# A graph transformer layer with a sparse expert step on one core: gap work, scatter-adds by halves, and a first expert product in three passes

## The chip, the cores and the metric

The kernel runs on one core of a Trainium2 chip. The metric is device time in microseconds. Engines are named as in the profile: PE (TensorE), PEld (its weight load), DVE (VectorE), ACT (ScalarE), POOL (GpSimd), SP (SyncE).

## The reference

1250 nodes of 768 features, 21,250 edges (self loops included). x is normalized (xn); to x are added a graph network and an attention by positive features, both of xn; then a layer of 8 experts, each token through its best two.

```python
# graph network, of xn
x_norm = layer_norm(x, norm_g, norm_b)
out1 = gat_conv(x_norm, src, dst, W1, a_src1, a_dst1, b1, 4, 192, n)   # 4 heads
out2 = gat_conv(out1, src, dst, W2, a_src2, a_dst2, b2, 2, 96, n)      # 2 heads
gnn = concat([x, out2]) @ Wu + bu
# gat_conv
h = (x @ W).reshape(n, H, C)
e = leaky_relu((h * a_src).sum(-1)[src] + (h * a_dst).sum(-1)[dst], 0.2)
ee = exp(e - segment_max(e, dst)[dst])
out = segment_sum(ee / segment_sum(ee, dst)[dst] * h[src], dst)
# experts, y = layernorm(x)
p = softmax(y @ router_w.T);  top 2, divided by a balance, normalized
out = sum over the two experts of gate * silu(y @ w1[e].T) @ w2[e].T
x = x + out
```

## The kernel before, in words

Nodes are kept as NT = 10 tiles of 128. The graph's edges become a dense table of counts, `cnt[st]` (source tile x 1280 targets, uint16), built by indirect scatter-adds on POOL. A product in fp32r takes three passes, `mm3`: hi x hi, hi x lo, lo x hi, where `hi` is the fp32r copy of an operand (ACT) and `lo` what is left (DVE, a subtract); a plain `mm` is in fp32. Eight PSUM banks go round in the order of `reserve` (line 302); `take`, `finished` and `evacuated` are the waits on them.

Ahead of the first attention PE computes h1 in 2 x 10 tiles (line 1855 on), half by half, with W1 folded and scaled by the gain. The second half's weights (`A0 + 1`) are split by `split_gain_hi` (ACT) and `split_gain_lo` (DVE, after the bias product `wb`). Between the h1 tiles PE turns the count table into mask tiles (`mask_tile`, at `PEN_AT`), which ACT makes into `pen[dt]`. For each head h and target tile dt, DVE takes the largest score over the sources, `masked_max`, with two inputs from SBUF: the row of scores `a_row[h]` and `pen[dt]`. Tiles 0 to 3 are taken for all four heads at once, tiles 4 to 9 head by head. `leaky_max` makes of them two columns per target; PE turns these (`max_rows`), DVE copies the result (`mrow`), POOL writes it to `m_d` and reads it back spread over all partitions (`u1_row`, `u2_row`). The rows of head 0 stand where `a_row[1]` and `a_row[2]` were, so they can be loaded only after the maxima of these heads. ACT takes an offset off the ten `cnt` tiles after the last h1 tile.

An attention (DVE's `attention`, line 1353) goes over heads and source tiles: ACT makes `vbuf`, DVE `pbuf` (line 1373), ACT the exponential, DVE times the counts (line 1399), PE ten products for `aggregate` (line 1890). `pbuf` has three buffers. `bank_out` divides a finished head.

Between the attentions PE spreads the new score rows (`aR`), turns Wu's lower part (`wuT`), multiplies it by the router (`wuR`), sums the router (`rsum`), and then takes x1 tile by tile through the router, with `spread_shifts` for the two heads of the second attention; meanwhile DVE does its 20 maxima.

The expert stage has NP_ = 27 tiles of up to 128 rows, each of one expert, `owner[a]`. A tile a: POOL fetches its rows of y from DRAM (`ygot`, line 718), PE turns them (`turn_rows`), ACT copies them (`ygT`), PE multiplies them by the owner's W1 out of `f1_all` (group `F`, 256 columns, fp32), ACT does silu, PE turns the hidden rows (`hT`), DVE copies them (`hgT`), PE multiplies by W2 (group `S`, two halves of 384), DVE scales by the gate into `orow`, and POOL adds these rows to `out` by an indirect DMA (line 728). An addition waits until the one before has landed, since two tiles can hold the same row of `out`. Ahead of it stands a routing part on DVE that makes the lists `fetch`, `send`, `owner` and the gates.

## Time and profile before

| | us |
|---|---|
| median of 3 runs (lowest, highest) | 1066.67 (1063.98, 1069.22) |
| profiled execution, its own time | 1061.51 |
| its span | 1059.8 |
| PE busy | 925.7 (87%) |
| DVE busy | 627.1 (59%) |
| POOL busy | 389.6 (37%) |
| ACT busy | 386.2 (36%) |

The profile is of one execution; the 1.7 us beside the span lie around it. In the chain that ended last PE has 53%, DVE 20%, DMA 16%, waiting for nothing that shows 6%. The mean granted clock of PE is 0.935 of full speed. In the rows below, times are from the span's start; "[x <-E name Ln]" is idle time of the engine ahead of the row and who ended it.

### The profile page before, as it was taken

Reading aid. Unit: us, or ns where it says so; the run is one execution under the profiler, and the core shown is the slowest. Engines: PE = TensorE matmul, PEld = TensorE weight load, DVE = VectorE, ACT = ScalarE, POOL = GpSimd, SP = SyncE. Lnnn points to the kernel's source line nnn. Section 1 sums busy time; section 2 is a strip of 40 time slices with the busy share of each in tenths; the row PEclk is TensorE's granted clock in tenths of the full one; section 3 lists DMA queues with packets and bytes.
Section 4 is the critical chain, followed back from the end, with each engine's and each line's share of the span. In section 5 each row is a group of like instructions: output and inputs, shape, how many; then the busy total and the mean of one; then the engine's idle time right before and its main releaser. Section 6 shows DMA issues by size and latency. Waiting matters only on the chain.

```text
span 1059.8 us, 13855 instructions
## 1 busy us (share of the span) xinstructions
PE 925.7 (87%) x5064; PEld 785.8 (74%) x5064; DVE 627.1 (59%) x1222; ACT 386.2 (36%) x575; POOL 389.6 (37%) x302
## 2 busy tenths in 40 slices
PE   3899899999999999999189999897888469999993
PEld 3798785786678899999088988886877457666672
DVE  7676995602078132386989999695996763222221
ACT  2543330223344000244576766346863401121120
POOL 3058888888888874000110000000000313434441
PEclk9999999969999999999589999989988759999997
DMA  9994579333226449600140000216005924666664
GB/s 315 232 161 83 96 203 263 51 45 45 1 1 145 63 92 287 200 2 1 51 149 23 1 1 1 88 63 208 2 1 199 363 60 91 119 120 119 120 120 60
DMA packets 78417, 112.43 MB, mean 106 GB/s; under 512 B 34994, under 2 KB 53933, under 8 KB 78351
## 3 DMA queue, kind: packets, MB, share of 16 engines
q0 software_dynamic: 35264, 39.86, 22.9%
q1 hardware_dynamic: 40781, 65.39, 19.2%
q10 hardware_dynamic: 2306, 6.29, 1.5%
q8 instruction: 42, 0.69, 0.3%
q14 instruction: 24, 0.20, 0.1%
HBM read 80.02 MB, written 31.49 MB: 105 GB/s over the span
## 4 chain that ended last, share of the span: by engine, by line
PE 53%; DVE 20%; DMA 16%; issue 6%; ACT 2%; SPq 1%; POOL 0%; POOLq 0%; DVEq 0%; ACTq 0%
PE bank L1621 41%; DMA out<-orow,send 14%; PE bank L1890 9%; DVE pbuf L1399 4%; DVE pbuf L1373 3%; DVE sb_before L1318 3%; DVE junk_k L1194 2%; PE bank L1632 2%; DVE h L1382 2%; DMA keyrow<-key_d 2%; SPq L552 1%; DVE o L1382 1%; PE bank L1826 0%; DVE sb_stats L1142 0%; DVE xnT_lo L1118 0%
## 5 line engine op out<-in xcount | busy, mean ns | idle before, releaser
L661 POOL DMA_INDIRECT table<-match_n,slot_ix x168 | 276.2, 1644 | 90.2 <-issue 48.9
L1890 PE MATMUL bank<-h,pbuf 128*128 128x197 f32 (+1 forms) x1200 | 194.5, 324 | 29.6 <-DVE pbuf L1399 28.6
L1890 PEld LDWEIGHTS bank<-h,pbuf 128*128 128x128 f32 x1200 | 186.7, 199 | 37.4 <-DVE pbuf L1399 34.2
L1194 DVE SCALAR_TENSOR_TENSOR junk_k<-keyrow,key,sb_before 128x384 uint8<-128x384 f32 x168 | 92.7, 614 | 21.8 <-DMA keyrow<-key_d 11.5
L1318 DVE CUSTOM_DVE_ANT_0 sb_before<-a_row,pen 128x1280 bf16<-128x1280 f32 x60 | 89.4, 1491 | 27.3 <-ACT pen L958 11.2
L1606 DVE TENSOR_SCALAR orow<-bank,gates 128x384 f32<-128x384 f32 x54 | 33.4, 618 | 115.8 <-PE bank L1621 115.8
L692 POOL IOTA cst_i<- 128x128 int32 x1 | 0.2, 229 | 271.8 <-DVE o L1382 271.8
L1016 ACT ACTIVATE pbuf<-pbuf 128x1280 f32<-128x1280 f32 x60 | 76.1, 1269 | 64.4 <-DVE pbuf L1373 64.4
L1399 DVE SCALAR_TENSOR_TENSOR pbuf<-pbuf,cnt 128x1280 f32<-128x1280 f32 x60 | 88.7, 1485 | 0.0
L1621 PE MATMUL bank<-xnT_hi,w_hi 128*128 128x512 f32 (+1 forms) x216 | 85.1, 394 | 3.7 <-DVE xnT_lo L1118 2.8
L728 POOL DMA_INDIRECT out<-orow,send x27 | 42.9, 1587 | 111.5 <-DMA out<-orow,send 92.5
L1621 PE MATMUL bank<-w_hi,xnT_hi 128*128 128x384 f32 x240 | 82.3, 343 | 0.0
L1621 PE MATMUL bank<-w_hi,xnT_lo 128*128 128x384 f32 x240 | 80.7, 336 | 0.0
L1621 PE MATMUL bank<-w_lo,xnT_hi 128*128 128x384 f32 x240 | 80.5, 336 | 0.0
L1621 PE MATMUL bank<-xnT_lo,w_hi 128*128 128x512 f32 (+1 forms) x216 | 78.3, 363 | 0.0
L1621 PE MATMUL bank<-xnT_hi,w_lo 128*128 128x512 f32 (+1 forms) x216 | 78.2, 362 | 0.0
L1621 PE MATMUL bank<-f_all,ygT 128*128 x324 | 77.0, 389 | 1.2 <-issue 0.7
L1621 PE MATMUL bank<-f_all,hgT 128*128 x216 | 74.3, 487 | 1.3 <-DVE hgT L1587 1.3
L1373 DVE SCALAR_TENSOR_TENSOR pbuf<-u_row,sb_scol,vbuf 128x1280 f32<-128x1280 f32 x40 | 61.7, 1550 | 12.7 <-PE bank L1890 12.3
L1621 PEld LDWEIGHTS bank<-f_all,ygT 128*128 128x128 f32 x324 | 61.1, 195 | 9.5 <-issue 1.9
L815 ACT ACTIVATE kq<-bank,sb_kqb_c 128x512 f32<-128x512 f32 (+1 forms) x36 | 22.2, 617 | 112.0 <-PE bank L1621 104.6
L1098 ACT ACTIVATE hrow<-bank 128x256 f32<-128x256 f32 x27 | 10.4, 384 | 131.2 <-PE bank L1621 131.2
(346 smaller groups left out, 1668.4 us busy)
## 6 DMA issues: line engine op xcount, KB each, us to landing
...
```

What stands on the lines that cost most here:

```text
L661: pool.indirect_dma_start(table[i], bass.IndirectOffsetOnAxis(ap=slot_ix[:, g:g + 1], axis=0), match_n[:, g:g + 1], None, compute_op=ALU.a ...
L728: pool.indirect_dma_start(out, bass.IndirectOffsetOnAxis(ap=send[:, a:a + 1], axis=0), orow[a % 3][:, :], None, compute_op=ALU.add, bounds ...
L815: step(nc.scalar.activation(kq[j % 2][0][:, 0:w], b[:, 0:w], ACT.Identity, bias=kqb_c[:, col:col + 1]))
L1016: nc.scalar.activation(pbuf[i % 3][:, :], pbuf[i % 3][:, :], ACT.Exp).then_inc(e_done, 1)
L1194: nc.vector.scalar_tensor_tensor(out=junk_k[g % 2][:, :], in0=keyrow[c % KR][:, w:w + KW * P], scalar=key[:, g:g + 1], in1=before[:, first ...
L1318: ins = nc.vector.tensor_tensor_reduce(out=junk_m[:, :], in0=rows_a[h][:, :], in1=pen_t[:, :], scale=1.0, scalar=-3e38, op0=ALU.subtract, ...
L1373: nc.vector.scalar_tensor_tensor(out=pbuf[i % 3][:, :], in0=u1_r[h][:, :], scalar=scol[:, h, st:st + 1], in1=vbuf[i % 2][:, :], op0=ALU.ad ...
L1382: ins = nc.vector.scalar_tensor_tensor(out=out_rows(h, per * i + d), in0=pv[:, d, 0:chans], scalar=rec[:, d:d + 1], in1=added(h, per * i + ...
L1399: nc.vector.scalar_tensor_tensor(out=pbuf[i % 3][:, :], in0=pbuf[i % 3][:, :], scalar=2.0, in1=cnt[st][:, :], op0=ALU.min, op1=ALU.mult).t ...
L1606: ins = nc.vector.tensor_scalar(orow[a % 3][:, hf * HALF:(hf + 1) * HALF], b[:, 0:HALF], gates[:, a:a + 1], None, ALU.mult)
L1621: return nc.tensor.matmul(o, l, r, start=first, stop=last)
L1890: ins = nc.tensor.matmul(b[:, d * stride:d * stride + v.shape[-1]], score[:, dt * P:(dt + 1) * P], v, start=st == 0 and d == 0, stop=st == ...
```

## The change

Ahead of the first attention: mask tiles are made at other h1 tiles, two at a time from the second half on; DVE takes tiles 4 to 9 for heads 0 and 1 together, then for head 2, and head 3's six maxima go into the first attention (`between_first`), as do the sums for the layer's bias. Head 3's shift columns go to `m_d` by a DMA of SP straight from `ucol`. The low part of W1's second half is made by POOL in two passes, and so is the low part of Wu. ACT's work on `cnt` is spread over the second half of h1. Between the attentions: `wuT` and `rsum` come ahead of the `aR` spreads, and ACT takes the second head's shift rows after the attention's third and fourth tiles. In the expert stage: ACT and DVE split the owner's W1 (`own_hi`, `own_lo`) and the turned rows (`ygT_hi`, `ygT_lo`) for every tile, the first product goes through `mm3`, and each tile's rows are added in two indirect DMAs of 384 columns, each waiting for the same half of the tile before.

```diff
+        ygT_hi = [at(f"ygT_hi{i}", (181664, 105472)[i], [P, KD, P], F32R) for i in range(2)]
+        ygT_lo = [at(f"ygT_lo{i}", 61440 + 3072 * i, [P, KD, P], F32R) for i in range(2)]
...
+        own_hi = [at(f"own_hi{i}", (108544, 76800)[i], [P, KD, FI], F32R) for i in range(2)]
+        own_lo = [at(f"own_lo{i}", (114688, 82944)[i], [P, KD, FI], F32R) for i in range(2)]
...
-        PEN_AT = [(0, 2), (0, 4), (0, 7), (0, 8), (1, 0), (1, 1), (1, 2), (1, 3), (1, 4), (1, 5)]
-        ROWS_AT = {(1, 6): 0, (1, 9): 1}
+        PEN_AT = {(0, 2): [0], (0, 3): [1], (0, 4): [2], (0, 6): [3], (1, 0): [4, 5], (1, 1): [6, 7], (1, 2): [8, 9]}
+        ROWS_AT = {(1, 5): 0, (1, 6): 1, (1, 8): 2}
+        LESS_AT = {(1, 3): [0], (1, 4): [1, 2], (1, 5): [3], (1, 6): [4, 5], (1, 7): [6], (1, 8): [7, 8], (1, 9): [9]}
...
+            sp.wait_ge(m_done, H1)
+            sp.dma_start(m_d[2 * (H1 - 1) * NT:2 * H1 * NT, :].rearrange("(k t) p -> p k t", k=2), ucol[:, H1 - 1, :, :],
+                         allow_slow_non_contiguous=True).then_inc(m_out[H1 - 1], 16)
...
+            pool.wait_ge(w_hi_done, SPLITS.index(A0 + 1) + 1)
+            finished(pool, "wb", 1)
+            i, gain = SLOT[A0 + 1], gb_c[:, 0, :].unsqueeze(2).broadcast_to([P, KD, HALF])
+            nc.gpsimd.tensor_tensor(w_raw[i][:, :, :], w_raw[i][:, :, :], gain, ALU.mult).then_inc(gain_done, 1)
+            pool.wait_ge(gain_done, 1)
+            ins = nc.gpsimd.tensor_tensor(w_lo[i][:, :, :], w_raw[i][:, :, :], w_hi[i][:, :, :].bitcast(F32), ALU.subtract)
+            ins.then_inc(w_split, 1)
             for h in range(H1):
-                evacuated(pool, "mT", h)
-                pool.dma_start(m_d[2 * h * NT:2 * (h + 1) * NT, :], mrow[h % 2][:, :]).then_inc(m_out[h], 16)
                 if h == 2:
+                    pool.wait_ge(max_done, NT + NT - 4)
                     pool.dma_start(u1_row[0][:, :], row_of(m_d, 0)).then_inc(u_row_in[0], 16)
                     pool.dma_start(u2_row[0][:, :], row_of(m_d, 1)).then_inc(u_row_in[0], 16)
-                pool.wait_ge(m_out[h], 16)
+                if h < H1 - 1:
+                    evacuated(pool, "mT", h)
+                    pool.dma_start(m_d[2 * h * NT:2 * (h + 1) * NT, :], mrow[h % 2][:, :]).then_inc(m_out[h], 16)
+                if h < H1 - 1:
+                    pool.wait_ge(m_out[h], 16)
             finished(pool, "h1", 1, NT - 1)
...
+                if h == H1 - 1:
+                    pool.wait_ge(m_out[h], 16)
                 pool.dma_start(u1_row[h][:, :], row_of(m_d, 2 * h)).then_inc(u_row_in[h], 16)
                 pool.dma_start(u2_row[h][:, :], row_of(m_d, 2 * h + 1)).then_inc(u_row_in[h], 16)
 
+            pool.wait_ge(g_hi_done, 1)
+            nc.gpsimd.tensor_tensor(wuo_lo[:, :, :], wuo_raw[:, :, :], wuo_hi[:, :, :].bitcast(F32), ALU.subtract).then_inc(g_split, 1)
...
+            def send_rows(a, hf):
                 if a == 0:
                     pool.wait_ge(send_done, 1)
                     pool.wait_ge(out_sent, 16 * NT)
                 else:
-                    pool.wait_ge(added_out, 16 * a)
-                pool.wait_ge(orow_done, 2 * (a + 1))
-                pool.indirect_dma_start(out, bass.IndirectOffsetOnAxis(ap=send[:, a:a + 1], axis=0), orow[a % 3][:, :], None,
-                                        compute_op=ALU.add, bounds_check=N - 1).then_inc(added_out, 16)
+                    pool.wait_ge(added_out[hf], 16 * a)
+                pool.wait_ge(orow_done, 2 * a + hf + 1)
+                pool.indirect_dma_start(half_rows, bass.IndirectOffsetOnAxis(ap=send[:, hf, a:a + 1], axis=0),
+                                        orow[a % 3][:, hf * HALF:(hf + 1) * HALF], None,
+                                        compute_op=ALU.add, bounds_check=2 * N - 1).then_inc(added_out[hf], 16)
...
+                    if (hf, t) == (0, 4):
+                        split_gain_hi(act, A0 + 1)
                     if (hf, t) == (0, 5):
-                        split_gain_hi(act, A0 + 1)
-                    if (hf, t) == (0, 6):
                         weight_rows(1)
-            for i in range(NT):
-                nc.scalar.activation(cnt[i][:, :], cnt[i][:, :], ACT.Identity, bias=less_c[:, 0:1]).then_inc(cnt_done, 1)
+                    for i in LESS_AT.get((hf, t), ()):
+                        nc.scalar.activation(cnt[i][:, :], cnt[i][:, :], ACT.Identity, bias=less_c[:, 0:1]).then_inc(cnt_done, 1)
...
-            rows_out("uR2", (0,), 1, u1_row_b[1])
-            rows_out("uR2", (1,), 1, u2_row_b[1])
-            act.wait_ge(max_done, MAX1 + 2 * NT)
-            attention(H1, H2, u2_row_b, row_ready_2)
+            act.wait_ge(max_done, MAX1 + NT)
+
+            def rows_between(i):
+                if i in (2, 3):
+                    rows_out("uR2", (i - 2,), 1, (u1_row_b, u2_row_b)[i - 2][1])
+
+            attention(H1, H2, u2_row_b, row_ready_2, rows_between)
...
+            def own_weights(a):
+                if a >= 2:
+                    finished(act, "F", a - 2)
+                e = act.value_load(owner[0:1, a:a + 1], min_val=0, max_val=E - 1)
+                nc.scalar.activation(own_hi[a % 2][:, :, :].rearrange("p k n -> p (k n)"),
+                                     f1_all[:, bass.DynSlice(e, 1), :, :].rearrange("p o k n -> p (o k n)"), ACT.Copy).then_inc(own_hi_done, 1)
...
+            own_weights(0)
             turned_rows(0)
+            act.wait_ge(out_sent, 16 * NT)
+            own_weights(1)
...
+                if a + 2 < NP_:
+                    own_weights(a + 2)
...
-                if dt == 0:
-                    for h in range(H1):
-                        dve.wait_ge(a_in[h], 16)
                 masked_max(pen[dt], a_row, range(H1), dt)
-                if dt == 1:
-                    split_gain_lo(dve, A0 + 1)
-            for h in range(H1):
-                for dt in range(4, NT):
-                    if h == 0:
-                        evacuated(dve, "pen", dt, 0), evacuated(dve, "pen", dt, 1)
-                    masked_max(pen[dt], a_row, (h,), dt)
-                dve.wait_ge(max_done, 4 + (h + 1) * (NT - 4))
-                leaky_max(H1, h, 1)
+            def max_row_out(h):
                 b = finished(dve, "mT", h)
                 if h >= 2:
                     dve.wait_ge(m_out[h - 2], 16)
                 nc.vector.tensor_copy(mrow[h % 2][:, :], b[0:2 * NT, 0:P]).then_inc(free("mT", h), 1)
...
+            for dt in range(4, NT):
+                evacuated(dve, "pen", dt, 0), evacuated(dve, "pen", dt, 1)
+                masked_max(pen[dt], a_row, (0, 1), dt)
+            dve.wait_ge(max_done, NT)
+            leaky_max(H1, 0, 1), leaky_max(H1, 1, 1)
+            for dt in range(4, NT):
+                if dt == 7:
+                    max_row_out(0), max_row_out(1)
+                masked_max(pen[dt], a_row, (2,), dt)
+            dve.wait_ge(max_done, NT + NT - 4)
+            leaky_max(H1, 2, 1)
+
+            def between_first(i):
+                if i == 0:
+                    max_row_out(2)
+                if i == 1:
+                    bias_of_layer()
+                if i % 3 == 2 and i < 18:
+                    masked_max(pen[4 + i // 3], a_row, (3,), 4 + i // 3)
+                if i == 18:
+                    dve.wait_ge(max_done, MAX1)
+                    leaky_max(H1, 3, 1)
+
...
-            dve.wait_ge(g_hi_done, 1)
-            nc.vector.tensor_tensor(wuo_lo[:, :, :], wuo_raw[:, :, :], wuo_hi[:, :, :].bitcast(F32), ALU.subtract).then_inc(g_split, 1)
...
+            def low_rows(a):
+                if a >= 2:
+                    finished(dve, "F", a - 2)
+                for h in range(2):
+                    b = finished(dve, "yT", a, h)
+                    dve.wait_ge(y_hi_done, 2 * a + h + 1)
+                    s = slice(3 * h, 3 * h + 3)
+                    nc.vector.tensor_tensor(ygT_lo[a % 2][:, s, :], transposed(b, h), ygT_hi[a % 2][:, s, :].bitcast(F32),
+                                            ALU.subtract).then_inc(free("yT", a, h), 1)
+
+            def own_low(a):
+                e = dve.value_load(owner[0:1, a:a + 1], min_val=0, max_val=E - 1)
+                dve.wait_ge(own_hi_done, a + 1)
+                nc.vector.tensor_tensor(own_lo[a % 2][:, :, :].rearrange("p k n -> p (k n)"),
+                                        f1_all[:, bass.DynSlice(e, 1), :, :].rearrange("p o k n -> p (o k n)"),
+                                        own_hi[a % 2][:, :, :].rearrange("p k n -> p (k n)").bitcast(F32), ALU.subtract).then_inc(own_done, 1)
...
+            dve.wait_ge(owner_done, 1)
+            own_low(0)
...
+            low_rows(0)
...
+            own_low(1)
...
             for a in range(NP_ + 1):
+                if a + 1 < NP_:
+                    low_rows(a + 1)
                 if a:
                     expert_rows(a - 1)
                 if a < NP_:
                     turned_hidden(a)
+                if a + 2 < NP_:
+                    own_low(a + 2)
...
-                    if (hf, t) in PEN_AT:
-                        mask_tile(PEN_AT.index((hf, t)))
-                    if (hf, t) == (0, 6):
+                    for dt in PEN_AT.get((hf, t), ()):
+                        mask_tile(dt)
+                    if (hf, t) == (0, 5):
                         bias_rows(1)
                     if (hf, t) in ROWS_AT:
                         max_rows(ROWS_AT[hf, t])
-            max_rows(2), max_rows(3)
...
-            pe.wait_ge(dots_done, 2)
-            for h in range(H2):
-                spread_row("aR", (), h, scol[:, h, :])
-
...
+            pe.wait_ge(mean_done, 2)
+            b = take(pe, "rsum")
+            for m in range(KD):
+                ins = mm(b[:, 0:EM], ones[:, :], rw_raw[:, m, :], m == 0, m == KD - 1)
+            ins.then_inc(full("rsum"), 1)
+            pe.wait_ge(dots_done, 2)
+            for h in range(H2):
+                spread_row("aR", (), h, scol[:, h, :])
             evacuated_all(pe, "wuT")
-            pe.wait_ge(mean_done, 2)
...
-            b = take(pe, "rsum")
-            for m in range(KD):
-                ins = mm(b[:, 0:EM], ones[:, :], rw_raw[:, m, :], m == 0, m == KD - 1)
-            ins.then_inc(full("rsum"), 1)
...
+                    pe.wait_ge(own_done, a + 1)
                     b = take(pe, "F", a)
                     for k in range(KD):
-                        ins = mm(b[:, 0:FI], ygT[a % 2][:, k, :], f1_all[:, bass.DynSlice(e_of[a], 1), k, :], k == 0, k == KD - 1)
+                        ins = mm3(b[:, 0:FI], [z[a % 2][:, k, :] for z in (ygT_hi, ygT_lo)],
+                                  [z[a % 2][:, k, :] for z in (own_hi, own_lo)], k == 0, k == KD - 1)
                     ins.then_inc(full("F", a), 1)
```

POOL ahead of the first attention, before: the four writes of the shift columns and the loads of the rows.
```order
L681 DMA m_d<-sb_mrow 20x128 [waits bank_free5]
L681 DMA m_d<-sb_srow 20x128 [waits bank_free1,m_out0]
L681 DMA m_d<-sb_mrow 20x128 [waits bank_free2,m_out1]
L683 DMA u_row_137<-m_d 128x1280
L684 DMA u_row_141<-m_d 128x1280
L681 DMA m_d<-sb_srow 20x128 [waits bank_free3,m_out2]
L688 DMA u_row_138<-m_d 128x1280 [waits bank_full0,m_out3]
L689 DMA u_row_142<-m_d 128x1280
```
And now (`w_raw_84` and `w_lo_81` are the second half of W1, one place in memory):
```order
L690 TENSOR_TENSOR w_raw_84<-w_raw_84,sb_gb_c 128x2304 [waits bank_full3,w_hi_done]
L692 TENSOR_TENSOR w_lo_81<-w_raw_84,w_hi_78 128x2304 [waits gain_done]
L701 DMA m_d<-sb_mrow 20x128 [waits bank_free4]
L701 DMA m_d<-sb_srow 20x128 [waits bank_free6,m_out0]
L697 DMA u_row_137<-m_d 128x1280 [waits max_done,m_out1]
L698 DMA u_row_141<-m_d 128x1280
L701 DMA m_d<-sb_mrow 20x128 [waits bank_free1]
L708 DMA u_row_138<-m_d 128x1280 [waits bank_full2,m_out2]
L709 DMA u_row_142<-m_d 128x1280
```
Two passes over W1 stand ahead of the writes, the first load comes ahead of head 2's write, head 3's write is gone from POOL, and Wu's pass follows after the loads (not shown).

PE between the attentions, before, from the last products of the first attention on:
```order
L1890 MATMUL bank<-h_105,pbuf_147 128x197 x10
L1621 MATMUL bank<-sb_ident,sb_scol 128x128 x20
L1910 MATMUL bank<-sb_ident,wuo_raw 128x96 x12
L1621 MATMUL bank<-sb_rw_raw,wuoT 96x10 x12
L1621 MATMUL bank<-sb_rw_raw,sb_ones 128x10 x6
L1632 MATMUL bank<-sb_ident,x_165 128x128 x12
```
And now:
```order
L1977 MATMUL bank<-h_105,pbuf_147 128x197 x10
L1993 MATMUL bank<-sb_ident,wuo_raw 128x96 x12
L1712 MATMUL bank<-sb_rw_raw,sb_ones 128x10 x6
L1712 MATMUL bank<-sb_ident,sb_scol 128x128 x20
L1712 MATMUL bank<-sb_rw_raw,wuoT 96x10 x12
L1723 MATMUL bank<-sb_ident,x_165 128x128 x12
```
The transposes of Wu and the router's sum moved ahead of the spreads of `sb_scol`.

DVE at the first two tiles of the expert stage, before:
```order
L1587 COPY hgT_224<-bank 128x256
L1592 SCALAR_TENSOR_TENSOR list_f<-bank,list_f 128x27
L1594 TENSOR_TENSOR list_f<-list_f,bank 128x27
L1595 CAST send<-list_f 128x27
L1598 TENSOR_REDUCE gates<-bank 128x27
L1606 TENSOR_SCALAR orow_226<-bank,gates 128x384 x2
L1587 COPY hgT_225<-bank 128x256
```
And now (`TENSOR_LOAD` reads the owner into a register):
```order
L1673 COPY hgT_222<-bank 128x256
L1600 TENSOR_LOAD owner
L1600 ISA x2
L1602 ISA
L1602 TENSOR_TENSOR own_lo_233<-f_all,own_hi_231 128x1536
L1596 TENSOR_TENSOR ygT_lo_226<-bank,ygT_hi_224 128x384 x2
L1678 SCALAR_TENSOR_TENSOR list_f<-bank,list_f 128x27
L1680 TENSOR_TENSOR list_f<-list_f,bank 128x27
L1681 TENSOR_SCALAR send<-list_f 128x27
L1682 TENSOR_SCALAR send<-list_f 128x27
L1685 TENSOR_REDUCE gates<-bank 128x27
L1693 TENSOR_SCALAR orow_228<-bank,gates 128x384 x2
```
Ahead of each tile's `orow` there is now the low part of an owner's weights and that of the next tile's rows.

## Rows read from the trace of the kernel before

**Rows 1.** DVE's timeline ahead of the first attention: start, us, engine, line, operation, out<-in, count.
```profile
444.92 1.49 DVE L1318 CUSTOM_DVE_ANT_0 sb_before<-a_row,pen 128x1280 bf16<-128x1280 f32 x1 [9.31 <-DMA a_row<-s_d]
...
446.45 1.49 DVE L1318 CUSTOM_DVE_ANT_0 sb_before<-a_row,pen 128x1280 bf16<-128x1280 f32 x1
...
528.43 0.54 DVE L1410 TENSOR_TENSOR sb_row_t<-sb_row_t 128x384 f32<-128x384 f32 x1
...
529.99 3.02 DVE L1373 SCALAR_TENSOR_TENSOR pbuf<-u_row,sb_scol,vbuf 128x1280 f32<-128x1280 f32 x2
```

**Rows 2.** ACT's and POOL's timelines there, with idle time before and its releaser.
```profile
472.83 0.59 ACT L953 ACTIVATE h<-bank,sb_rs 128x384 f32<-128x384 f32 x1 [2.54 <-PE bank L1621]
...
524.82 2.61 ACT L1007 ACTIVATE vbuf<-u_row,sb_a 128x1280 f32<-128x1280 f32 x2 [5.99 <-DMA u_row<-m_d]
...
518.87 0.56 POOL L683 DMA_DIRECT2D u_row<-m_d  x1
...
531.30 0.55 POOL L688 DMA_DIRECT2D u_row<-m_d  x1 [1.72 <-DMA m_d<-sb_srow]
```

**Rows 3.** POOL's line L708 (min/median/max ns), and one DVE row beside it.
```profile
L708 POOL TENSOR_SCALAR yrow<-x,sb_of_tokens,sb_rs x10: 973/976/1067, 835.3 to 844.1; 128x768 f32<-128x768 f32 x10
...
838.37 0.91 DVE L1474 TENSOR_TENSOR sb_of_tokens<-sb_of_tokens 128x80 f32<-128x80 f32 x1
```

**Rows 4.** Windows of the first two heads: us, busy of PE, PEld, DVE, ACT, POOL, clock, DMA.
```profile
530.00:567.00 37.00, 32.54 (x182) 32.41 (x183) 30.97 (x22) 26.84 (x22) 3.19 (x6) 0.88 0.29 107
567.00:604.00 37.00, 34.61 (x202) 33.01 (x201) 34.12 (x36) 25.07 (x21) 0.00 (x0) 1.00 0.06 17
```

**Rows 5.** PE's, ACT's and DVE's timelines between the attentions.
```profile
691.03 1.16 PE L1910 MATMUL bank<-sb_ident,wuo_raw 96*128 96x96 f32 x12
...
693.24 2.18 PE L1621 MATMUL bank<-sb_rw_raw,wuoT 128*96 128x10 f32 x24 [1.06 <-ACT wuoT L1028]
...
697.29 2.80 PE L1632 MATMUL bank<-sb_ident,x 128*128 128x128 f32 x12
...
727.82 0.25 ACT L1049 ACTIVATE sb_lr<-bank 128x100 f32<-128x100 f32 x1 [0.45 <-PE bank L1947]
...
721.64 1.77 DVE L1432 TENSOR_TENSOR wuo_lo<-wuo_raw,wuo_hi 96x1556 fp32r<-96x1556 f32 x1
...
734.30 3.01 DVE L1373 SCALAR_TENSOR_TENSOR pbuf<-u_row_b,sb_scol,vbuf 128x1280 f32<-128x1280 f32 x2 [10.88 <-ACT vbuf L1007]
```

**Rows 6.** PE's timeline, one tile of the expert stage.
```profile
1031.78 0.87 PE L1632 MATMUL bank<-sb_ident,ygot 128*128 128x128 f32 x6 [0.16 <-DMA ygot<-y_d,fetch]
1032.49 2.75 PE L1621 MATMUL bank<-f_all,hgT 128*128 x8
1035.07 0.38 PE L2038 MATMUL bank<-sb_ident,hrow 128*128 128x128 f32 x2
1035.29 2.75 PE L1621 MATMUL bank<-f_all,ygT 128*128 x12
1037.88 2.74 PE L1621 MATMUL bank<-f_all,hgT 128*128 x8
```

**Rows 7.** POOL's first and last send; time to landing of the sends, then of the fetches.
```profile
880.90 1.64 POOL L728 DMA_INDIRECT out<-orow,send  x1 [14.63 <-DVE orow L1606]
...
1050.40 1.56 POOL L728 DMA_INDIRECT out<-orow,send  x1 [4.54 <-DMA out<-orow,send]
...
DMA to landing us min/median/max: 5.3/5.5/6.3
...
DMA to landing us min/median/max: 4.5/5.1/5.8
```

**Rows 8.** PE's timeline, two fp32r matmuls over 256 columns, the second 12 after the first.
```profile
123.67 0.28 PE L1621 MATMUL bank<-xnT_hi,w_hi 128*128 128x256 f32 x1
...
125.05 0.28 PE L1621 MATMUL bank<-xnT_hi,w_hi 128*128 128x256 f32 x1
```

**Rows 9.** DVE's timeline ahead of the dummy rows' marks.
```profile
871.05 0.17 DVE L1574 TENSOR_TENSOR spot<-bank,used_of 128x8 f32<-128x8 f32 x1 [5.68 <-PE bank L1621]
```

112 lines of the change are left out of this document (62 added, 50 removed).

## The prediction

> **What bounds the kernel now.** I read the chain of waits first, then the timelines of DVE, ACT, POOL and PE around its gaps. Three stretches are in play. (1) Ahead of the first attention, DVE is alone on the path: the first of its 40 row maxima starts at 444.92 and the next 1.53 later; the first pbuf is only made at 529.99 [rows 1]. (2) Between the attentions PE works through transposes, and the second attention starts at 734.30, though DVE's maxima had ended at 721.64 [rows 5]. (3) In the expert stage 27 scatter-adds follow each other, each held until the one before has landed: the first starts at 880.90, the last at 1050.40, 26 steps of 6.52 us [rows 7]. PE needs 0.71 (turn) + 2.58 (second product) + 0.22 + 2.59 (first product) = 6.10 us a tile [rows 6], so it is almost as tight. A shorter send alone would gain 0.4 us a tile: both have to move.
>
> **The first gap.** Gains:
> - Head 3's six maxima leave the gap (6 x 1.53 = 9.2 us), and DVE's split of the second half of the folded W1 goes to POOL.
> - Mask tiles come earlier. Before, maxima of tiles 4 to 9 went to one head each time a tile came. Now two heads use each, and tiles 4 to 9 arrive in three pairs.
>
> Working: DVE starts at about 443.5 (it now waits for one score row, not four, and the first mask). 16 maxima take 24.6: 468.1. Tile 4 cannot come before the h1 tile copied at 472.83 [rows 2] plus 0.5 for that copy and 1.5 for the two mask halves: about 474.5. Against this stands POOL's work: 2 passes over 2304 columns. The nearest row is its one-input pass over 768 columns, 0.976 us [rows 3]; scaled by 3 it is 2.9 a pass, doubled for two inputs 5.9; I take 4.4, so 8.8 for both, with ends 5.9 and 11.8. While POOL ran those passes, a DVE operation with two inputs over 80 columns took 0.91 us [rows 3], more than half of what one over 1280 takes [rows 1]: DVE stood behind POOL. I let DVE lose all of the 8.8: 468.1 + 8.8 = 476.9, only 2.4 behind the 474.5 at which the masks would have stopped it anyway. Then 12 maxima (18.4), eight small steps of 0.17 [rows 9] and 0.03 between them (1.6), 3 maxima (4.6) and two row copies (0.6): 502.1. Two writes of m_d follow, each 0.5 to issue and 1.72 until seen landed [rows 2], 0.4 between: 507.1 for the load of the first shift row, which before was issued at 518.87. ACT could start 5.95 later [rows 2], and its pass takes 1.3: the first pbuf at 514.4, against 529.99. That is -15.6, with ends -18 (POOL harmless) and -12.6 (11.8 us lost). PE is not late: max_rows(2) waits until about 507.5, one h1 tile follows, and ACT's ten subtractions from cnt, which stood behind it, are spread over the earlier tiles.
>
> The Trainium skill speaks here, against the change: "SBUF — State Buffer", section "Who interferes with whom", says a VectorE instruction with two SBUF inputs and a GpSimd one that reads SBUF exclude each other for the whole instruction. By that rule, the stretched DVE row fits, and the maxima (two SBUF inputs) lose all of POOL's time. The skill's "GPSIMD Engine Reference", section "Elementwise — side-by-side cycle accounting", has 4497 ns for 2048 columns of tensor_tensor; as an estimate that is 5.1 a pass, and the start would be 1.3 later.
>
> What is given back: head 3's maxima (9.2), its small steps (0.8), the bias sums (528.43 to 529.99, 1.6 [rows 1]) and a row copy (0.2) now lie inside the attention, 11.8 in all. In the first head's window DVE was busy 30.97 of 37, so 6 are free; in the second's 34.12 of 37, so 2.9 are free, but only in its second half [rows 4]. 6.4 fall in head 0: hidden. 5.4 fall in head 1, of which I hide 1.4: +4, ends +1.5 and +7. **First gap: -11.6**, ends -16 and -6.
>
> **The second gap.** PE ends the row spreads at 691.03, then does the wuT transposes, waits for ACT's copies until 693.24, does 24 products and then 12 for rsum, and starts on x1 at 697.29 [rows 5]. Transposes and rsum now stand before the spreads, in PE's wait for DVE, and the wait for the copies goes; 24 products remain (2.0): x1 starts at 693.1, -4.2. ACT's copy of lr moves from 727.82 to 723.6. The second head's spreads stood between it and the attention; ACT now takes them after tiles 2 and 3, so the first pbuf can come at 723.6 + 0.25 + 1.35 = 725.2, against 734.30: -9.1. DVE's maxima ended at 721.64 [rows 5]; POOL's subtract of Wu, 1556 columns (2.0 to 4.0 by the same scaling), falls on them and can push them to 725.6: what would be late next. ACT's two extra sets (2.7) lie in tiles where it has little room: +1.5. **Second gap: -7.3**, ends -9 and -4.
>
> **The expert stage.**
> - First product: 12 fp32 passes (2.59) become 18 of fp32r. The 256-column fp32r matmuls start 12 per 1.38 us [rows 8]: 18 take 2.08, so PE's tile is 5.59.
> - Send: half the bytes each. The 384 KB send lands 5.5 us after its issue (median) and at most 1.0 passes until the next issue [rows 7]; since many landings lie above the median I count 0.8. Half may cost the same 5.5, or, if all but POOL's 1.6 scales, 3.6. Period by this chain: 4.4 to 6.3. I take a landing of 4.5.
> - POOL: two issues of 1.6 and a fetch of 1.1 with 0.3 each: 5.2 a tile. Not the bound, but the fetch now stands behind two sends. Loop: the first half of the second product ends 4.1 into PE's tile, orow 0.8, two sends 3.8: fetch issued at 8.7; it lands 5.1 later [rows 7], 13.8; its rows are turned 2 tiles and 2.1 later. 2T + 2.1 = 13.8, T = 5.85. This is above PE's 5.59 and I take it.
> - DVE per tile: low rows 2 x 0.55, orow 2 x 0.6, hgT 0.4, own_low 1536 columns at 1.77 per 1556 [rows 5] and a register load of some 0.4: 4.9 of 5.85. ACT: the hi copy of 1536 columns 1.6 (its passes over 1280 take 1.3 [rows 2]) beside silu and the row copies. Both fit.
>
> 26 x (6.52 - 5.85) = -17.4. The start gets later: DVE idled 5.68 before 871.05 [rows 9]; the inserted own_low(0) with its wait for ACT (3.8), low_rows(0) (1.1) and own_low(1) (2.1) use this up and 1.3 more, and PE's F(1), formerly done before the dummies' marks, now waits for low_rows(1) behind them: F(1), a turn, the lists and half a product follow, first send near 884.2, +3.3. The last tile has a second send, +0.9. **Expert stage: -13**, ends -19 (T = 5.6) and +1 (T = 6.35).
>
> The Trainium skill's "DMA: Bandwidth & Descriptors", section "Anatomy of one DMA", makes most of a transfer's time fixed (2.0 us and bytes/436e3): by that rule halving the send saves only 0.45 us, landing 5.05, chain 5.9. No run here shows a half send yet; the sum would hardly move.
>
> **Sum.** -11.6 - 7.3 - 13 = -32 on the profiled execution of 1061.51 (span 1059.8 and 1.7 around it). That execution is 5 us under the median of the runs, 1066.67; the same difference taken from the median gives **1035**.
>
> **Rivals.**
> 1. *The half send takes as long as the whole one.* For it: landing varies only from 5.3 to 6.3 whatever else moves [rows 7]. Period 5.5 + 0.83 = 6.33; the stage gives 26 x 0.19 = 4.9, less 4.2: -1. Total -20: 1047. Chance 0.22.
> 2. *POOL's passes hurt more*: slow (11.8 us and over) and holding up both the maxima and PE's second half of h1; Wu's subtract pushes the second gap. First gap -6, second -4, experts -13: 1044. Chance 0.15.
> 3. *Everything fits*: PE bound tail (5.6), no blocking: -16 - 9 - 19 = -44: 1023. Chance 0.13.
> 4. *Slower.* POOL becomes the bound of the expert stage: its issues are stretched by DVE's new 1536-column pass, which has two SBUF inputs, in every tile. It decides when the tile's period passes 6.52 + (19 - 4)/26 = 7.1, since the gaps give 19 and the stage's ends take 4: that is when each of the three issues takes 0.63 more than now. At 1 us more each the period is 8.2, the stage costs 44 + 4, and the total is +29: 1096. Against it: PE, ACT and DVE keep 1 us of room, and POOL's issue of the sends varies little. Chance 0.03.
> 5. *The gaps do not shrink*, since PE's h1 or the mask copies set the end, and the tail is rival 1's: -4: 1063, no change. Chance 0.03.
>
> Forecast itself 0.44. The range 1021 to 1052 leaves out rivals 4, 5 and the outer part of 1. A measurement tells about 0.5% (5 us) from no change: faster 0.93, same 0.04, slower 0.03.
>
> **What would show it.** First pbuf of attention 1 at 514 (right) or past 520 (POOL's passes longer or PE late); DVE maxima of over 1.5 us, or gaps between them, while POOL multiplies. Attention 2's first pbuf 9 us nearer to the end of attention 1. In the tail the start-to-start time of sends of one half: 5.85 with PE waiting for ygot; 5.6 without such waits; 6.3 with POOL waiting for `out`. Landing of a half send: 4.5, or 5.5. If sends step at 6.3, the forecast fails there; if the first attention starts at the old distance, the order of maxima was not the bound.

## The result, and the profile after

The changed kernel takes 1061.28 us (median of 4 runs, 1060.94 to 1061.71), the kernel before 1067.14 us (4 runs): ratio 0.9948, 95% interval 0.9922 to 0.9973. It is faster, by 6 us and not by the forecast 32. The profiled execution after has a span of 1059.0 us, the one before had 1059.8; that execution, 1061.51 us by its own time, lay below all four timed runs of its kernel (1063.98 to 1069.22), which is why the two traces differ by less than the medians do.

The gain is there, and it is given back. Places on the path in both traces (us):

| place | before | after | difference |
|---|---|---|---|
| first row maximum of layer 1 | 444.92 | 446.54 | +1.6 |
| first pbuf of attention 1 | 529.99 | 518.77 | -11.2 |
| end of attention 1 (copy to sb_scol) | 684.37 | 679.43 | -4.9 |
| first pbuf of attention 2 | 734.30 | 722.12 | -12.2 |
| POOL's first yrow pass | 835.27 | 823.49 | -11.8 |
| first row addition | 880.90 | 875.18 | -5.7 |
| last tile's first row addition | 1050.40 | 1047.71 | -2.7 |
| end of the span | 1059.8 | 1059.0 | -0.8 |

The gaps brought 11.8 us, and the expert stage gave 11.0 of it back.

**Ahead of attention 1.** The rows that answer to [rows 1, 2], DVE's timeline, then POOL's (start, us, engine, line, operation, out<-in, count):

```profile
446.54 1.49 DVE L1364 CUSTOM_DVE_ANT_0 sb_before<-a_row,pen 128x1280 bf16<-128x1280 f32 x1 [7.97 <-ACT pen L983]
...
460.64 5.20 DVE L1364 CUSTOM_DVE_ANT_0 sb_before<-a_row,pen 128x1280 bf16<-128x1280 f32 x1
...
465.88 6.34 DVE L1364 CUSTOM_DVE_ANT_0 sb_before<-a_row,pen 128x1280 bf16<-128x1280 f32 x1
...
518.77 3.01 DVE L1434 SCALAR_TENSOR_TENSOR pbuf<-u_row,sb_scol,vbuf 128x1280 f32<-128x1280 f32 x2 [7.29 <-ACT vbuf L1031]
```

```profile
459.70 4.79 POOL L690 TENSOR_TENSOR w_raw<-w_raw,sb_gb_c 128x2304 f32<-128x2304 f32 x1 [46.85 <-PE bank L1712]
464.57 6.30 POOL L692 TENSOR_TENSOR w_lo<-w_raw,w_hi 128x2304 fp32r<-128x2304 f32 x1
...
511.22 0.58 POOL L697 DMA_DIRECT2D u_row<-m_d  x1 [2.99 <-DVE sb_mxc L1364]
```

Two maxima that take 1.49 us elsewhere take 5.20 and 6.34 us, 8.6 us more, and each ends 1.35 us after the POOL pass beside it (465.84 after 464.49, 472.22 after 470.87). The passes took 4.79 and 6.30 us where 4.4 each was assumed. The second one began at 464.57, while a maximum was under way until 465.84, so part of its length may be POOL standing still for DVE; no run tests that. The trace agrees with the rule of the Trainium skill that the prediction cited ("SBUF — State Buffer", "Who interferes with whom").

ACT's row for [rows 2] and, of PE, the wait that is new here:

```profile
500.17 0.39 PE L1915 MATMUL bank<-sb_ident,ucol 128*20 128x128 f32 x1 [5.24 <-DVE ucol L1376]
```

```profile
517.27 2.61 ACT L1031 ACTIVATE vbuf<-u_row,sb_a 128x1280 f32<-128x1280 f32 x2
```

PE stands for 5.24 us until the maxima of head 0 are known. The load of the shift rows is issued at 511.22 (507.1 had been worked out), behind the last maximum of head 2, and ACT starts 6.05 later.

**Between the attentions**, the rows that answer to [rows 5]: ACT's copy of lr and DVE's first pbuf; then POOL's subtract of Wu and the maximum beside it.

```profile
720.37 0.25 ACT L1074 ACTIVATE sb_lr<-bank 128x100 f32<-128x100 f32 x1 [0.45 <-PE bank L2033]
```

```profile
722.12 3.02 DVE L1434 SCALAR_TENSOR_TENSOR pbuf<-u_row_b,sb_scol,vbuf 128x1280 f32<-128x1280 f32 x2 [3.54 <-ACT vbuf L1031]
```

```profile
688.52 4.04 POOL L712 TENSOR_TENSOR wuo_lo<-wuo_raw,wuo_hi 96x1556 fp32r<-96x1556 f32 x1 [75.15 <-ACT wuo_hi L1059]
```

```profile
689.26 4.65 DVE L1364 CUSTOM_DVE_ANT_0 sb_before<-a_row,pen 128x1280 bf16<-128x1280 f32 x1
```

The second attention starts 42.7 us behind the end of the first, 49.9 before. The maximum lost 3.2 us, and DVE still ended its maxima and their small steps (718.6) ahead of the copy of lr at 720.37, which lets the attention start.

**The expert stage.** POOL's timeline over two tiles; it answers to [rows 7]:

```profile
888.05 1.58 POOL L752 DMA_INDIRECT out<-orow,send  x1 [1.47 <-DVE orow L1693]
889.94 2.82 POOL L752 DMA_INDIRECT out<-orow,send  x1 [0.30 <-issue]
893.06 1.09 POOL L740 DMA_INDIRECT ygot<-y_d,fetch  x1 [0.30 <-DVE orow L1693]
894.46 1.58 POOL L752 DMA_INDIRECT out<-orow,send  x1 [0.31 <-DVE orow L1693]
896.34 2.06 POOL L752 DMA_INDIRECT out<-orow,send  x1 [0.30 <-issue]
898.70 1.09 POOL L740 DMA_INDIRECT ygot<-y_d,fetch  x1 [0.30 <-issue]
```

And DVE's own_lo passes beside them, then the turn of the rows on PE:

```profile
889.57 1.76 DVE L1602 TENSOR_TENSOR own_lo<-f_all,own_hi 128x1536 fp32r<-128x1536 f32 x1 [0.34 <-issue]
891.25 1.02 DVE L1596 TENSOR_TENSOR ygT_lo<-bank,ygT_hi 128x384 fp32r<-128x384 f32 x2
...
895.21 1.76 DVE L1602 TENSOR_TENSOR own_lo<-f_all,own_hi 128x1536 fp32r<-128x1536 f32 x1 [0.33 <-issue]
```

```profile
897.62 0.88 PE L1723 MATMUL bank<-sb_ident,ygot 128*128 128x128 f32 x6 [1.83 <-DMA ygot<-y_d,fetch]
```

The second addition of each tile is issued while DVE makes own_lo. The pass ends at 891.33 and the issue 1.43 later; the next pass ends at 896.97 and its issue again 1.43 later. So it is for the first 24 tiles, 1.42 to 1.46 us behind the pass each time. Undisturbed an issue takes 1.55. The fetch stands behind it, so it is issued late, lands 4.5 later (median), and PE waits. The whole stretch of PE's waits for fetched rows (880 to 1045), its rows of the view of waits, after and then before:

```profile
PEld bank L1723 <- DMA ygot<-y_d,fetch: 26.3, 19, 3.0
...
PE bank L1723 <- DMA ygot<-y_d,fetch: 22.2, 17, 2.8
```

```profile
PEld bank L1632 <- DMA ygot<-y_d,fetch: 14.8, 22, 1.3
...
PE bank L1632 <- DMA ygot<-y_d,fetch: 5.7, 12, 0.9
```

(Columns: total us, times, longest.) From 875.18 the additions step 6.64 us over 26 tiles, 6.52 before.

At the stage's start DVE no longer idles ahead of the dummy rows' marks [rows 9], but PE waits twice for DVE's low parts of the rows, which stand behind other work in DVE's queue:

```profile
856.04 0.55 PE L1712 MATMUL bank<-own_hi,ygT_hi 128*128 128x256 f32 x1 [3.45 <-DVE ygT_lo L1596]
...
866.24 0.55 PE L1712 MATMUL bank<-own_hi,ygT_hi 128*128 128x256 f32 x1 [5.15 <-DVE ygT_lo L1596]
```

### The profile page after: what moved, and what is told of

It reads as the page before. It is cut to its first block, busy times and chain, and to the rows that moved or that the text cites. A ratio compares the mean times of both kernels' runs of the same rounds, so it can differ in the third digit from the quotient of the medians.

```text
span 1059.0 us, 14522 instructions
## 1 busy us (share of the span) xinstructions
PE 912.8 (86%) x5225; PEld 786.2 (74%) x5225; DVE 706.8 (67%) x1296; ACT 425.5 (40%) x602; POOL 467.4 (44%) x331
## 4 chain that ended last, share of the span: by engine, by line
PE 46%; DVE 28%; DMA 10%; issue 8%; ACT 3%; POOL 3%; SPq 1%; POOLq 0%; DVEq 0%; ACTq 0%
PE bank L1712 37%; DVE sb_before L1364 7%; PE bank L1977 6%; DVE pbuf L1460 5%; DMA ygot<-y_d,fetch 5%; DVE pbuf L1434 4%; DMA out<-orow,send 3%; POOL out L752 2%; DVE junk_k L1238 2%; PE bank L1723 2%; DMA keyrow<-key_d 2%; DVE h L1443 2%; ACT vbuf L1031 1%; SPq L556 1%; DVE orow L1693 1%
## 5 line engine op out<-in xcount | busy, mean ns | idle before, releaser
L1977 PEld LDWEIGHTS bank<-h,pbuf 128*128 128x128 f32 x1200 | 185.3, 197 | 40.9 <-DVE pbuf L1460 38.6
L752 POOL DMA_INDIRECT out<-orow,send x54 | 106.8, 1978 | 57.9 <-DVE orow L1693 44.7
L1364 DVE CUSTOM_DVE_ANT_0 sb_before<-a_row,pen 128x1280 bf16<-128x1280 f32 x60 | 101.2, 1687 | 14.2 <-ACT pen L983 8.0
L782 DVE TENSOR_TENSOR w_lo<-w_raw,w_hi 128x2304 fp32r<-128x2304 f32 x6 | 15.4, 2565 | 68.7 <-ACT w_hi L777 68.7
L978 ACT ACTIVATE h<-bank,sb_rs 128x384 f32<-128x384 f32 x20 | 11.7, 583 | 115.6 <-PE bank L1712 115.4
L1712 PE MATMUL bank<-own_hi,ygT_hi 128*128 128x256 f32 x162 | 49.6, 306 | 8.6 <-DVE ygT_lo L1596 8.6
L1712 PEld LDWEIGHTS bank<-f_all,hgT 128*128 128x128 f32 x216 | 39.4, 192 | 23.4 <-issue 2.2
L1315 DVE TENSOR_TENSOR ubuf<-ubuf,bank 128x384 f32<-128x384 f32 x20 | 11.1, 554 | 65.8 <-PE bank L1712 65.7
## 6 DMA issues: line engine op xcount, KB each, us to landing
f_all<-in_w2T SPq DMA_DIRECT2D x8, 768.0 KB, 11.8
```

The source lines that it names most:

```text
L752: pool.indirect_dma_start(half_rows, bass.IndirectOffsetOnAxis(ap=send[:, hf, a:a + 1], axis=0), orow[a % 3][:, hf * HALF:(hf + 1) * HALF] ...
L1364: ins = nc.vector.tensor_tensor_reduce(out=junk_m[:, :], in0=rows_a[h][:, :], in1=pen_t[:, :], scale=1.0, scalar=-3e38, op0=ALU.subtract, ...
L1712: return nc.tensor.matmul(o, l, r, start=first, stop=last)
L1977: ins = nc.tensor.matmul(b[:, d * stride:d * stride + v.shape[-1]], score[:, dt * P:(dt + 1) * P], v, start=st == 0 and d == 0, stop=st == ...
```

## The experiments

All ratios are to the kernel before, run on the same chip in the same sitting, with 95% intervals; the kernel before took 1067.26 us in the first group of four, 1067.66 in the second and 1063.29 in the third. The changed kernel did not run again in these sittings, so what a kernel gains on it is read from the two ratios. "Step" is the mean distance of the first addition of a tile over 26 tiles in the trace.

| kernel | us | ratio | step |
|---|---|---|---|
| changed kernel | 1061.28 | 0.9948 (0.9922 to 0.9973) | 6.64 |
| gaps_only | 1052.58 | 0.9845 (0.9820 to 0.9870) | 6.68 |
| tail_only | 1081.14 | 1.0136 (1.0115 to 1.0158) | 6.64 |
| half_fp32 | 1039.74 | 0.9745 (0.9721 to 0.9770) | 6.14 |
| own_low_two | 1045.45 | 0.9792 (0.9759 to 0.9825) | 6.10 |
| early_fetch | 1037.66 | 0.9709 (0.9670 to 0.9748) | 5.66 |
| whole_send | 1070.81 | 1.0034 (1.0014 to 1.0055) | 6.95 |
| half_fp32_early | 1035.71 | 0.9690 (0.9660 to 0.9720) | 5.99 |
| w1_low_dve | 1058.60 | 0.9923 (0.9895 to 0.9950) | 6.66 |
| early_w1 | 1026.93 | 0.9661 (0.9640 to 0.9682) | 5.65 |
| early_w1_start | 1025.62 | 0.9643 (0.9618 to 0.9668) | 5.69 |
| early_w1_start_rows | 1027.08 | 0.9655 (0.9627 to 0.9682) | 5.84 |
| own_low_two_early | 1030.32 | 0.9703 (0.9683 to 0.9724) | 5.56 |

**1. The change in its two halves.** gaps_only is the changed kernel with the expert stage of before; tail_only is the kernel before with the new expert stage. In the diff of the change these are the parts up to `between_second`, and the parts on ygT, own, orow and send.

> The two gap changes alone; the expert stage is the one of before. In the traces the first row pass of the fin stage (823.5 after, 835.3 before) stands 11.8 us earlier, while the end of the span stands only 0.8 us earlier. Theory A (the gaps gave 11.8 us and the new expert stage gave 11 of it back): 11 to 12 us below the kernel before, that is 1055.5, and 5 to 11 us faster than the changed kernel. Rival B (the expert stage runs as fast as its transfers let it, whenever it starts; the first part's gain would be lost in this kernel too): within 3 us of the changed kernel, 1061.

> The change of the expert stage alone, with the gaps of before. Theory A: the expert stage of the changed kernel is 5 to 11 us longer than that of before, so 1072 to 1078, slower. Rival B (the stage itself is no slower, and something of the gaps upsets it): 1067 or less, as before.

Measured: 1.55% faster and 1.36% slower. Theory A holds, a little larger than read from the traces: -14.7 and +13.9 us. The product of the two ratios is 0.998, near the 0.9948 of both together. The expert stage as changed is a loss of its own.

**2. Which part of the expert stage.** half_fp32 takes out the split and the three passes (and with them every own_hi, own_lo and ygT_lo):

```diff
-                        ins = mm3(b[:, 0:FI], [z[a % 2][:, k, :] for z in (ygT_hi, ygT_lo)],
-                                  [z[a % 2][:, k, :] for z in (own_hi, own_lo)], k == 0, k == KD - 1)
+                        ins = mm(b[:, 0:FI], ygT_hi[a % 2][:, k, :], f1_all[:, bass.DynSlice(e_of[a], 1), k, :], k == 0, k == KD - 1)
```

> The changed kernel, but the first product of each tile is the fp32 one of before: no split of W1 and of the rows, no three passes; the additions still go in two transfers. Theory A1 (VectorE's 1.76 us pass over two SBUF tiles, own_lo, holds up the issue of POOL's second transfer by 0.5 to 1.2 us and with it the fetch): every second transfer is issued in 1.6 us again, the step of a tile is the 6.10 us of TensorE or a little more, so 26 x (6.5 - 6.15), 9 us faster than the changed kernel: 1052. Rival A2 (three issues a tile with their gaps are too many, whatever VectorE does): the step stays at 6.4 or more and the time at 1060.

own_low_two keeps them and takes out only VectorE's pass:

```diff
-                if a + 2 < NP_:
-                    own_low(a + 2)
```

> The changed kernel, but own_lo (W1's low part) is worked out for the first two tiles only and then used again: that part of the computation is left out, the three passes and everything else stay. Theory A1: the second transfer's issue falls from 2.0 to 2.8 us to 1.6 us in each tile, the fetch comes earlier, and the step falls from 6.5 to 5.7 to 5.9 us: 1043. Rival A2 (number of issues, or the landing of the fetch at 4.5 us with four transfers in flight): the step stays at 6.3 or more: 1057 or above.

POOL's addition issues (min/median/max ns of line L752) in the changed kernel, then without the pass:

```profile
L752 POOL DMA_INDIRECT out<-orow,send x44: 1554/1584/2971, 881.2 to 1025.8; - x44
```

```profile
L752 POOL DMA_INDIRECT out<-orow,send x50: 1550/1556/1587, 880.7 to 1029.2; - x50
```

No issue above 1.59 us is left without the pass, and the step falls to 6.10: A1's mechanism is shown, A2 falls. Whether the pass might instead have held up DVE's own work on the tile can be read off, and it had not: where PE has waited for rows, the first addition is issued some 3.75 us behind their turn with the pass (897.62 to 901.37) and without it (920.48 to 924.22). The size differs from both expectations: half_fp32 gained 2.0% on the changed kernel, some 21 us, where 9 was expected (its stage also starts earlier, its first addition 20.2 us behind the first fetch, 28.2 in the changed kernel), and own_low_two gained 0.53 a tile, not 0.7: PE still waits for fetches there.

**3. The loop through the fetch.** early_fetch issues each fetch one tile ahead, with the same three buffers:

```diff
-            for a in range(NP_ + 3):
-                if a < NP_:
-                    fetch_rows(a)
+            for a in range(3):
+                fetch_rows(a)
+            for a in range(2, NP_ + 3):
+                if a + 1 < NP_:
+                    fetch_rows(a + 1)
```

> The changed kernel with POOL's order in the expert stage turned: the fetch of tile a+4 is issued before the two transfers of tile a instead of behind them. Theory A3 (the step of 6.5 us is a loop through the fetch: two issues, one of them stretched, stand in front of it, and TensorE waits for the rows): TensorE no longer waits for a fetch, and the step falls to what comes next, POOL's own three issues with one stretched, 1.58 + 2.8 + 1.09 + 3 x 0.30 = 6.4 us at most, 6.0 at least: 26 x 0.3, 8 us faster than the changed kernel: 1053. Rival A4 (only the loop bounds): the step falls to TensorE's 5.6 to 5.8 and the time to 1041. Rival A5 (POOL's issues alone are the bound already): no change, 1061.

Rival A4 was right: 1037.66, step 5.66. Windows of the middle of the stage (us, busy of PE, PEld, DVE, ACT, POOL, clock, DMA share, GB/s), changed kernel, then early_fetch:

```profile
890.00:1010.00 120.00, 103.36 (x598) 80.01 (x597) 78.01 (x107) 49.32 (x72) 91.58 (x53) 0.99 0.69 115
```

```profile
890.00:1010.00 120.00, 120.00 (x726) 95.81 (x725) 90.37 (x127) 55.28 (x84) 92.41 (x62) 1.00 0.81 136
```

PE is busy the whole time. One tile of it on PE, turn, second product, turn of h, first product, next turn:

```profile
935.09 0.82 PE L1725 MATMUL bank<-sb_ident,ygot 128*128 128x128 f32 x6
935.75 2.75 PE L1714 MATMUL bank<-f_all,hgT 128*128 x8
938.33 0.38 PE L2128 MATMUL bank<-sb_ident,hrow 128*128 128x128 f32 x2
938.47 0.36 PE L1714 MATMUL bank<-own_hi,ygT_hi 128*128 128x256 f32 x1
...
940.67 0.82 PE L1725 MATMUL bank<-sb_ident,ygot 128*128 128x128 f32 x6
```

5.58 us a tile, against 6.10 before [rows 6]. POOL's issues, which A3 took for the next bound, are not: 92 of 120 us. They are also less stretched: POOL is busy 4.4 us a tile in this window, 5.1 in the changed kernel, since more of the issues now miss DVE's pass.

**4. Where the stretched issue costs once the loop is broken.** own_low_two_early joins the two edits; all but the first two tiles' own_lo is left out.

> The changed kernel with the fetch a tile earlier and own_lo worked out for the first two tiles only (left out for the others). Theory A10 (with the loop through the fetch broken, the stretched issues cost nothing, since TensorE is busy all the time): the step stays at 5.66 us and the time at 1037, as with the earlier fetch alone. Rival (VectorE's pass still costs): step 5.5, 1033.

0.9703 beside early_fetch's 0.9709: no difference that can be measured, though the trace's step is 5.56 against 5.66, 2.6 us over 26 tiles. Of the 14 to 17 us that the pass cost in the changed kernel nothing measurable is left once the fetch no longer stands behind the stretched issue; the intervals leave room for some 5 us.

**5. One transfer with the split kept.** whole_send sends the whole row again.

```diff
-                    send_rows(a - 3, 0), send_rows(a - 3, 1)
+                    send_rows(a - 3)
```

> The changed kernel, but the rows are added in one transfer, as before; the split of W1 and rows and the three passes stay. The row additions follow one another, each waiting for the landing of the one in front. Theory A: VectorE's pass can now stretch this one issue too, and the landing (4.9 us behind the issue) comes on top, so the step is 6.5 to 7.3 and the time 1062 to 1080. Rival (the third issue was the burden and one transfer less relieves POOL): step 6.3, 1055.

Slower than before, as theory A had it. POOL's addition issue and its landing in it, then the landing of a half addition in early_fetch (min/median/max):

```profile
L749 POOL DMA_INDIRECT out<-orow,send x21: 1586/2009/2994, 883.6 to 1024.3; - x21
...
DMA to landing us min/median/max: 5.5/6.3/6.9
```

```profile
DMA to landing us min/median/max: 4.3/4.6/5.6
```

Half the bytes land 0.9 to 1.7 us sooner than the whole (5.5 before [rows 7], 6.3 here), and two halves run beside each other. The two transfers are the good part of the change. With the fp32 product on both sides, gaps_only (one transfer) and half_fp32 (two) show it too: 0.9845 and 0.9745, steps of 6.68 and 6.14.

**6. Half transfers, fp32 product and the earlier fetch.**

> Two half transfers and the fp32 first product, with the fetch issued ahead of the transfers. With the fp32 product the step was 6.14 us where TensorE's own work is 6.10, and TensorE waited 7.6 us in all for fetched rows. Theory A3: these waits go, the step is 6.10: 1 to 4 us faster than the same kernel without it, 1037. Rival: the transfers of tile a, one issue later now, become the last and the step is 6.2 or more: 1040 to 1043.

1035.71, step 5.99: 0.55% below half_fp32, a little more than expected. Most steps in this trace are 6.05, a little under the 6.10 taken for PE's own work, and the last three are shorter. Beside early_fetch (0.9709, with the split) it is 0.9690: the intervals overlap. The three passes make the step 0.33 us shorter, 8.6 us over 26 tiles, and the first addition comes 27.9 us behind the first fetch instead of 20.5, so the split is worth nothing that can be measured here.

**7. POOL's passes over W1 taken back.** w1_low_dve calls `split_gain_lo(dve, A0 + 1)` behind the maxima of tile 1, and POOL's two passes are gone.

> The changed kernel, but the low part of the second half of layer 1's W goes back from POOL (two passes, 4.79 and 6.30 us) to VectorE (six operations, 3.27 us). In the changed kernel's trace two of VectorE's maxima, 1.49 us elsewhere, take 5.20 and 6.34 us beside POOL's passes: 8.6 us more. Theory A6 (VectorE stands still while POOL multiplies, and its row of maxima leads to attention 1): attention 1 starts 8.6 - 3.3 = 5 us earlier, at 513.5 instead of 518.8, and 3 to 5 us of it are left at the end: 1057. Rival A7 (the start of attention 1 hangs on the rows' transfer and on TensorE's h1): no change, 1061.

The distance from the first maximum to the first pbuf was 85.1 us before, 72.2 after, and is 69.4 here: 2.8 us, not 5. Part of the 8.6 us turned into a new wait for ACT's masks:

```profile
478.89 1.49 DVE L1357 CUSTOM_DVE_ANT_0 sb_before<-a_row,pen 128x1280 bf16<-128x1280 f32 x1 [2.67 <-ACT pen L976]
```

The time, 0.9923, is not resolved from the changed kernel's.

**8. Together, and two smaller orders.** early_w1 is early_fetch and w1_low_dve. early_w1_start also moves ygT_lo of tiles 0 and 1 forward in VectorE's queue (the line for tile 1; that for tile 0 moves ahead of the gates in the same way):

```diff
             own_low(1)
+            low_rows(1)
```

early_w1_start_rows also has `ROWS_AT = {(1, 6): 0, (1, 7): 1, (1, 9): 2}`.

> The changed kernel with two edits together: the fetch a tile earlier, and W1's low part of layer 1 on VectorE. Theory: they stand in different stages, so their gains add: -23.6 and -2.7 us against the changed kernel, 1035. Rival: the first stage's gain only moves the clock's dips, and the sum is no better than the earlier fetch alone, 1037.7.

> The kernel early_w1, and VectorE's queue at the start of the expert stage reordered: ygT_lo of tile 0 ahead of the gates, ygT_lo of tile 1 ahead of the marks of the dummies. In the changed kernel's trace TensorE waits 3.45 and 5.15 us for these two. Theory A8 (the 6 us that the stage starts late are these two waits): the first row addition comes 22 to 24 us behind the first fetch instead of 28, and the time falls by 4 to 5 us: 1030. Rival: the marks and lists that come later in exchange hold the first rows up, and 1 us or nothing is left: 1034.

> The kernel early_w1_start, and TensorE turns the maxima of heads 0, 1 and 2 one place later among layer 1's products, so that it fills the 5.2 us for which it waits for them in the changed kernel's trace. Theory A9 (attention 1 starts when ScalarE has evacuated the last of layer 1's products, which that wait delays): attention 1 starts 2 to 3 us earlier and 1 to 2 us of it are left: 1028.5. Rival (the start hangs on the landing of the rows, 6 us behind VectorE's maxima): attention 1 starts when it did, 1030.

early_w1 reaches 0.9661. If the gains of the two stages add, 0.9709 x 0.9923 / 0.9948 = 0.9685 is expected, so the run fits that, but it does not show it: the second gain was not resolved by itself, and the intervals of 0.9661 and 0.9709 overlap. With the new start the first addition comes 24.8 us behind the first fetch instead of 27.8, as A8 said, but the time (0.9643) is not resolved from early_w1's, and the step is 0.04 longer. A9 fell: the first pbuf still comes 69.4 us behind the first maximum, and the view of waits names what is late in its place:

```profile
ACT vbuf L1026 <- DMA u_row<-m_d: 4.9, 1, 4.9
```

early_w1_start, 3.6% below the kernel before and 3% below the changed one, has the lowest time, though early_w1 and early_w1_start_rows are not resolved from it.

## Why the prediction was wrong

- **First gap.** Forecast -15.6 at the first pbuf, measured -11.2. Counted from DVE's first maximum it is -14.2 and -12.8; the rest is a front that differs between executions (the first maximum came between 440.0 and 448.6 us in the runs here). POOL's passes took 11.1 us, within the ends, and DVE lost 8.6 of them, where all of an assumed 8.8 was to be lost: the length and the share were both off, and that they cancel is luck. The load of the rows was issued 64.7 us behind the first maximum, 63.6 by the working, and it waited for head 2's last maximum, not for the two writes. PE's 5.24 us wait was not foreseen, but no loss from it shows: in early_w1_start_rows ACT is ready 4.9 us before the rows land, and the attention starts at the same distance.
- **Give-back in attention 1.** Forecast +4, ends 1.5 and 7; measured 6.3 (154.4 to 160.7 us). The answering windows of [rows 4]:

```profile
530.00:567.00 37.00, 34.86 (x204) 33.54 (x203) 35.13 (x33) 22.91 (x19) 0.00 (x0) 1.00 0.18 62
567.00:604.00 37.00, 32.18 (x186) 30.35 (x185) 35.58 (x41) 25.04 (x20) 0.00 (x0) 1.00 0.03 1
```

  DVE is busy 35 of 37 us in both: head 0 hid less than assumed. First gap in all: -4.9 of the forecast -11.6.
- **Second gap.** Forecast -7.3 in all. From the end of attention 1 to the second's first pbuf -9.1 was forecast and -7.2 came (49.9 to 42.7): ACT's copy of lr is 40.9 us behind that end, not 39.2. ACT's extra sets cost 0.4 in attention 2, not 1.5 (101.0 to 101.4 us to the yrow pass). Sum -6.8: right, by two terms that missed in opposite directions. The working's own terms, -9.1 and +1.5, make -7.6, not -7.3. POOL's subtract, which might have been late next, stretched one maximum and delayed nothing on the path.
- **Expert stage: the step that failed.** "POOL: two issues of 1.6 and a fetch of 1.1 with 0.3 each ... Loop: ... 2T + 2.1 = 13.8, T = 5.85." The product and the transfers were sized well: PE's tile 5.58 (forecast 5.59), half addition landing in 4.6 (4.5), fetch in 4.5 (5.1). The loop was the right bound too. What was wrong is above all the second issue: 2.38 us in the mean, up to 2.97, in place of 1.6. The loop can be laid beside the trace, from one turn that waited for its rows to the next such turn, two tiles on:

| part of the loop (us) | worked out | own_low_two | changed kernel |
|---|---|---|---|
| turn to first addition's issue | 2.8 | 3.74 | 3.67 |
| both additions' issues, to the fetch's issue | 3.8 | 3.75 | 5.01 |
| fetch's issue to the next turn that waited | 5.1 | 4.51 | 4.56 |
| half the sum | 5.85 | 6.00 | 6.62 |

```profile
884.38 0.87 PE L1723 MATMUL bank<-sb_ident,ygot 128*128 128x128 f32 x6 [1.76 <-DMA ygot<-y_d,fetch]
```

```profile
920.48 0.87 PE L1721 MATMUL bank<-sb_ident,ygot 128*128 128x128 f32 x6 [0.92 <-DMA ygot<-y_d,fetch]
...
924.22 1.59 POOL L752 DMA_INDIRECT out<-orow,send  x1 [1.90 <-DVE orow L1693]
...
927.97 1.09 POOL L740 DMA_INDIRECT ygot<-y_d,fetch  x1 [0.30 <-issue]
...
932.48 0.87 PE L1721 MATMUL bank<-sb_ident,ygot 128*128 128x128 f32 x6 [0.50 <-DMA ygot<-y_d,fetch]
```

  The first line is of the changed kernel (its others stand above: 888.05, 893.06, 897.62), the rest of own_low_two. The mean steps are 6.64 and 6.10. The stretched issue gives 1.2 us of the loop, 0.6 a tile. A second term was short as well: from the turn to the first addition's issue 3.7 us pass, not 2.8; the shorter landing of the fetch takes back 0.6 of those 0.9. Instead of -17.4 the steps gave +3.0.
- **Start of the stage.** Forecast +3.3, measured +6.0: PE's two waits for ygT_lo; reordering them gave back 3.0 in the trace. The end: +0.9 forecast, +1.9 measured.
- **Slips in the working.** The stage's worse end, T = 6.35, gives 26 x 0.17 less 4.2, -0.2 and not +1, and 472.83 + 0.5 + 1.5 is 474.8, not 474.5. Neither moves the forecast.
- **The rivals.** Number 4 named the mechanism (POOL's issues stretched by DVE's 1536-column pass) and gave it 0.03, because it was priced as POOL's own period, which would have to pass 7.1 us, with all three issues stretched. It needed neither: one stretched issue in front of the fetch was enough, since POOL's delay enters a loop that had no slack. Number 1 is refuted (a half lands in 4.6, not 5.5).

The prediction cited a rule for the maxima and left it out of the loop's issues, though rival 4 had raised the point. The rule would not have settled it: the same section of the Trainium skill ("SBUF — State Buffer", "Who interferes with whom") gives the exclusion for a GpSimd instruction that reads SBUF, and says that a probe had not seen `tensor_tensor` stall a DMA. Here a pass of that kind, own_lo, does hold up the issue of a DMA on POOL, by 0.5 to 1.4 us, and the measurement decides. Both directions are now in the traces: in the gap DVE waits for POOL, in the expert stage POOL waits for DVE.
